# Gating the summed states of a state-space layer on VectorE instead of POOL, for seven of eight sequences

## The chip, the cores and the metric

One core of one Trainium2 chip runs the whole program. The metric is the device time in microseconds of one execution, from the first to the last instruction of the core with what lies around them.

## What is computed

The input holds eight sequences of 256 tokens with 128 features. Each sequence passes four blocks, each one added to its input after a layer norm: a selective state-space layer (Mamba), a mixture of eight experts of which two count for a token, a gated attention, and the same mixture of experts again. The change touches the end of the state-space layer, cut here to its core:

```python
conv = silu(sum(conv_w[k] * xp[:, k:k + T, :] for k in range(4)) + conv_b)
xpj = conv @ xproj_w                       # gives ts, Bm and Cm
delta = softplus(ts @ dt_w + dt_b)
gate_a = silu(gate)                        # gate is the second half of xn @ in_w + in_b
def step(state, inp):                      # one token; 16 states for each of 256 channels
    h_t, d_t, g_t, B_t, C_t = inp
    new = exp(A * d_t) * state + d_t * B_t * h_t
    y = sum over the 16 states of new * C_t, plus D * h_t
    return new, y * g_t
x = x + ssm @ out_w + out_b
```

The product `y * g_t` is what this document calls gating.

## The kernel before, in words

**Tiles.** The channels lie on the 128 partitions in two halves and the 256 tokens along the free axis, so that one tile of a sequence's layer is 128x512 in 32-bit floats. The time recurrence of one state is one scan instruction over such a tile.

**One sequence's states.** For each of the 16 states n of sequence u:

- VectorE (DVE) multiplies delta times h by the broadcast row of B (`dbx`, line 876, written to PSUM) and scans over time (`scan`, line 890, written to the ring `st` of three buffers in SBUF);
- GpSimd (POOL) multiplies the scanned state by the row of C (`mulC`, line 454);
- the product is added up: for sequence 0 on TensorE in PSUM (`NSUM` is 1), for sequences 1 to 7 on POOL in `yacc` in SBUF (`sum_states`, line 467).

`yacc` has two buffers, one for even and one for odd sequences, and is filled first with D times h by ScalarE (`m_y0`).

**After the sixteenth state.** `m_gate` multiplies the sum by `gact`, the silu of the gate half of the projection. For sequence 0 it stands on DVE and reads the sum from PSUM (line 899). For sequences 1 to 7 it stands on POOL (line 474). It counts up the semaphore `m_yg`. TensorE (PE) waits for that in `m_out` (lines 1091 and 1095), the output projection; DVE waits for the projection in `m_res` (line 903), which adds it to `X`. Behind `m_res` stand on DVE the norm of the next block (`n_stats`, line 797, with `n_ve` at line 915; `n_nb`, line 920; `n_lo`, line 927, which writes `xlo`). POOL's `n_pow` (line 413) and ScalarE stand between them. With `xlo` PE can begin the first mixture of experts of the sequence, line 1027. In DVE's queue around this place stand also `combine` (line 991, the weighted sum of experts of an earlier sequence), the first states of the next sequence, and the norm of the sequence after next (`m_stats`, with `m_ve` at line 810, and `m_nb`, line 815), for which POOL takes a power in `m_pow` (line 406).

**The order.** Each engine runs its instructions in order. `build_plan` gives every step of every sequence a planned moment, by tables written out by hand, sorts all steps by it, and each engine emits those steps that it has a function for. The table `M_OUT` plans `m_gate` 2.79, `m_out` 3.4 and `m_res` 5.45 after a common point. The step `m_gate` is in the plan of both DVE and POOL, and a function that returns at once emits nothing.

In the texts below "boundary u" is the place at which sequence u's sum is finished, gated and projected, u from 1 to 7.

Of the kernel before, what the change touches and what calls it, by code (L numbers as in the profile page):

```python
# [5 lines left out]
ALU = mybir.AluOpType  # L6
# [13 lines left out]
NS = 16  # L20
# [14 lines left out]
NSUM = 1  # L35
# [149 lines left out]
def build(nc, x, vecs, in_w, xproj_w, dt_w, out_w, gate_w, up_w, down_w, uv_w, wo_w, row_b, router_w, out):  # L185
    schedule = build_plan()
    norms = norm_order(schedule)
    with ExitStack() as ctx:
        def sb(name, shape, dt=F32):
            return ctx.enter_context(nc.sbuf_tensor(name, shape, dt))  # L190

        def two(bank):
            return bank.rearrange("p (a t) -> p a t", a=2)

        ps = ctx.enter_context(nc.psum_tensor("ps", [P, 8, 512], F32))
        s = {n: ctx.enter_context(nc.semaphore(n)) for n in SEMS}
        bc = nc.dram_tensor("bc", (S, 2 * NS * T), F32).ap()

        rot = [ps[:, k, :] for k in range(NR)]
# [43 lines left out]
        gact = sb("gact", [P, IT, T])  # L243
# [9 lines left out]
        yacc = sb("yacc", [P, 2, IT, T])  # L253
# [45 lines left out]
        def v(col, n=1):  # L299
            return vec[:, col:col + n]  # L300
# [12 lines left out]
        def run_schedule(share):  # L313
            for name, arg in schedule:
                if name in share:
                    share[name](arg)
# [4 lines left out]
        def _(sp):  # L321
            def setup(_):
                def seq(k, n):
                    return x[k * T:(k + n) * T, :].rearrange("(s c p) h -> p (s c) h", c=NC, p=P)

                def tiles(k, n):
                    return X[:, k:k + n].rearrange("p s c h -> p (s c) h")

                sp.dma_start(tiles(0, 1), seq(0, 1)).then_inc(s["d_x0"], 16)
                sp.dma_start(in_raw, in_w).then_inc(s["d_inw"], 16)  # L330
                sp.dma_start(vec[:], vecs).then_inc(s["d_vecs"], 16)
                for sem, dst, src in (("d_xpw", xpw[:], xproj_w), ("d_dtw", dtw[:], dt_w), ("d_outw", outw[:], out_w)):
                    sp.dma_start(dst, src).then_inc(s[sem], 16)
                for k in (0, LOW):
                    sp.dma_start(rowb_raw[k:k + 1, :], row_b).then_inc(s["d_rowb"], 16)
                sp.dma_start(tiles(1, S - 1), seq(1, S - 1)).then_inc(s["d_xs"], 16)
                sp.dma_start(gate_raw, gate_w).then_inc(s["d_gate"], 16)
                sp.dma_start(up_raw, up_w).then_inc(s["d_up"], 16)
                for sem, dst, src in (("d_rw", rw_raw[:], router_w), ("d_uv", uv_raw, uv_w), ("d_wo", wo[:], wo_w)):
                    sp.dma_start(dst, src).then_inc(s[sem], 16)  # L340

            def load_down(_):
                for k in range(NB):
                    rows = min(P, FI - k * P)
                    sp.dma_start(down[0:rows, :, k, :],
                                 down_w[:, k * P:k * P + rows, :].rearrange("e p h -> p e h")).then_inc(s["d_down"], 16)
# [43 lines left out]
        @block.gpsimd  # L390
        def _(pool):
            def setup(_):
                nc.gpsimd.memset(ident[:], 0.0).then_inc(s["w_zero"], 1)
                pool.wait_ge(s["w_zero"], 1)
                nc.gpsimd.affine_select(out=ident[:], in_=ident[:], compare_op=ALU.not_equal, fill=1.0, base=0,
                                        pattern=[[-1, P]], channel_multiplier=1).then_inc(s["w_const"], 1)
                nc.gpsimd.memset(neghalf[:], -0.5).then_inc(s["w_zero"], 1)
                nc.gpsimd.memset(one_at[:], 0.0).then_inc(s["w_zero"], 1)
                nc.gpsimd.iota(iota_i[:], pattern=[[1, NE]], base=0, channel_multiplier=0).then_inc(s["w_iota"], 1)
                pool.wait_ge(s["w_zero"], 3)  # L400
                nc.gpsimd.affine_select(out=one_at[:], in_=one_at[:], compare_op=ALU.not_equal, fill=1.0, base=-RK,
                                        pattern=[[0, 1]], channel_multiplier=1).then_inc(s["w_msk"], 1)

            def m_pow(u):
                pool.wait_ge(s["m_var"], u + 1)
                nc.gpsimd.tensor_tensor(m_r[:], m_ve[:], neghalf[:], ALU.pow).then_inc(s["m_rstd"], 1)

            def n_pow(arg):
                l = norms[arg]
                pool.wait_ge(s["n_var"], l + 1)  # L410
                if l:
                    pool.wait_ge(s["n_xm"], l)
                nc.gpsimd.tensor_tensor(n_r[:], n_ve[:], neghalf[:], ALU.pow).then_inc(s["n_rstd"], 1)  # L413

            def conv_product(k):

                def product(u):
                    if u == 0:
                        return
                    if k == 1:  # L420
                        pool.wait_ge(s["m_pad"], u + 1)
                    if u > 1 or k > 1:
                        pool.wait_ge(s["m_sum"], PAD * (u - 1) + k - 1)
                    w = v(V_CW, IT * KC).rearrange("p (a k) -> p a k", a=IT)[:, :, k:k + 1].broadcast_to([P, IT, T])
                    nc.gpsimd.tensor_tensor(tap[:], xpad[:, :, k:k + T], w, ALU.mult).then_inc(s["m_tap"], 1)  # L425
                return product

            def conv_sum(k):

                def tap_sum(u):  # L430
                    if u == 0:
                        return
                    pool.wait_ge(s["m_tap"], PAD * (u - 1) + k)
                    if k == 1:
                        pool.wait_ge(s["m_tap0"], u + 1)
                    nc.gpsimd.tensor_tensor(conv[:], conv[:], tap[:], ALU.add).then_inc(s["m_sum"], 1)  # L436
                return tap_sum

            def m_delta(u):
                if u == 0:  # L440
                    return
                pool.wait_ge(s["m_pos"], u + 1)
                pool.wait_ge(s["m_ln"], u + 1)
                pool.wait_ge(s["m_dA"], u * NS)
                pool.wait_ge(s["m_dx"], u)
                nc.gpsimd.tensor_tensor(delta[:], sp_e[:], sp_ln[:], ALU.add).then_inc(s["m_delta"], 1)  # L446

            def mulC(arg):

                u, n = arg  # L450
                i = u * NS + n
                pool.wait_ge(s["m_scan"], i + 1)
                row = rowsbc[:, (i // CH) % NCH, n % CH, 1:2, :].broadcast_to([P, IT, T])
                nc.gpsimd.tensor_tensor(st[:, i % NST], st[:, i % NST], row, ALU.mult).then_inc(s["m_p"], 1)  # L454

            def sum_states(arg):

                u, n = arg
                i = u * NS + n
                if u < NSUM:  # L460
                    return
                pool.wait_ge(s["m_p"], i + 1)
                if n == 0:
                    pool.wait_ge(s["m_y0"], u + 1)
                else:
                    pool.wait_ge(s["m_yacc"], i - NS * NSUM)
                nc.gpsimd.tensor_tensor(yacc[:, u % 2], yacc[:, u % 2], st[:, i % NST], ALU.add).then_inc(s["m_yacc"], 1)  # L467

            def m_gate(u):
                if u < NSUM:  # L470
                    return
                pool.wait_ge(s["m_yacc"], (u + 1 - NSUM) * NS)
                pool.wait_ge(s["m_g"], u + 1)
                nc.gpsimd.tensor_tensor(yacc[:, u % 2], yacc[:, u % 2], gact[:], ALU.mult).then_inc(s["m_yg"], 1)  # L474

            run_schedule({"setup": setup, "m_pow": m_pow, "n_pow": n_pow, "m_mul1": conv_product(1), "m_add1": conv_sum(1),
                          "m_mul2": conv_product(2), "m_add2": conv_sum(2), "m_mul3": conv_product(3), "m_add3": conv_sum(3), "m_delta": m_delta, "mulC": mulC,
                          "sum": sum_states, "m_gate": m_gate})

        @block.scalar  # L480
        def _(act):
# [9 lines left out]
            def setup(_):  # L491
                table("exp")
                act.wait_ge(s["d_vecs"], 16)
                nc.scalar.activation(A[:].rearrange("p a n -> p (a n)"), v(V_ALOG, IT * NS), ACT.Exp).then_inc(s["w_A"], 1)
# [241 lines left out]
        def _(dve):  # L736
# [155 lines left out]
                                             op1=ALU.add).then_inc(s["m_scan"], 1)  # L892

            def m_gate(u):
                if u >= NSUM:
                    return
                dve.wait_ge(s["m_ysum"], (u + 1) * NS)
                dve.wait_ge(s["m_g"], u + 1)
                nc.vector.tensor_tensor(yacc[:, u % 2], two(rot[0]), gact[:], ALU.mult).then_inc(s["m_yg"], 1)

            def m_res(u):
                dve.wait_ge(s["m_out"], u + 1)
# [406 lines left out]
```

## Time and profile before

| what | us |
|---|---|
| three timed runs | 674.55, 679.75, 679.70 |
| their median | 679.7 |
| the profiled execution, its own time | 673.82 |
| its span, first to last instruction | 672.2 |
| PE busy | 577.3 |
| DVE busy | 528.1 |
| POOL busy | 399.5 |
| ACT (ScalarE) busy | 383.3 |
| the 112 sums on POOL (line 467) | 143.8 |
| the 128 products with C on POOL (line 454) | 169.0 |

A timeline row has the start and the duration in microseconds, the engine, the line, the operation, what it writes and reads, and in brackets how long the engine sat idle before it and who released it. The chain of waits is followed backward from the last instruction: each piece is what released the next, and "issue" is time that no row explains. The granted clock of TensorE (PEclk) is a share of its full speed: 1.00 is 2.4 GHz, 0.50 is 1.2 GHz, and a value between them is a mean over a stretch that has both.

### The profile page before, as it was taken

What the parts mean: (1) busy time and instruction counts of PE and PEld (TensorE: products, weight loads), DVE (VectorE), ACT (ScalarE), POOL (GpSimd) and SP (SyncE); (2) the same over time, 40 slices, a digit from 0 to 9 for tenths busy, and PEclk for the clock granted to TensorE, in tenths of its full rate; (3) what the DMA queues carried; (4) which work ended last, traced back from release to release, by engine and by line L of the source; (5) the groups of instructions that cost most, each with busy time, mean ns of one, the idle gap of its engine ahead of it and who ended that gap; (6) DMA issues with size and microseconds to landing.
All of it is one profiled execution on the core that took longest, in us unless ns stands there. A gap on an engine that the chain in (4) does not pass through costs nothing.

```text
span 672.2 us, 12730 instructions
## 1 busy us (share of the span) xinstructions
PE 577.3 (86%) x4370; PEld 546.1 (81%) x4370; DVE 528.1 (79%) x1162; ACT 383.3 (57%) x792; POOL 399.5 (59%) x338
## 2 busy tenths in 40 slices
PE   2476792289798999999998999899989999999998
PEld 1222692289798999899898999899988999999998
DVE  6598899667799789988997799978988896545454
ACT  6886565257456675757573765667474641525240
POOL 1296599849667687759674986769775565000000
PEclk9588796569899999989997999999998999999999
DMA  8733033002030303021030303030303000000000
GB/s 294 222 123 125 11 131 119 7 20 120 1 138 9 138 4 137 2 90 59 13 126 14 133 3 138 9 138 3 127 13 121 25 13 1 22 1 13 1 21 9
DMA packets 18163, 45.30 MB, mean 67 GB/s; under 512 B 2800, under 2 KB 13489, under 8 KB 13747
## 3 DMA queue, kind: packets, MB, share of 16 engines
q1 hardware_dynamic: 18098, 44.49, 18.3%
q8 instruction: 35, 0.57, 0.4%
q14 instruction: 30, 0.24, 0.1%
HBM read 40.02 MB, written 1.31 MB: 61 GB/s over the span
## 4 chain that ended last, share of the span: by engine, by line
PE 37%; POOL 35%; issue 15%; DVE 8%; ACT 2%; DMA 1%; SPq 1%; POOLq 0%; DVEq 0%; ACTq 0%
POOL yacc L467 14%; POOL st L454 14%; PE ps L1178 9%; PE ps L1027 7%; PE ps L1028 7%; PE ps L1029 7%; POOL conv L436 2%; POOL tap L425 1%; DVE st L890 1%; DVE X L991 1%; PE ps L1227 1%; DMA inner_ring<-gate_w 1%; POOL delta L446 1%; POOL yacc L474 1%; DVE ps L876 1%
## 5 line engine op out<-in xcount | busy, mean ns | idle before, releaser
L454 POOL TENSOR_TENSOR st<-st,rows_ring 128x512 f32<-128x512 f32 x128 | 169.0, 1321 | 83.3 <-DVE st L890 83.0
L1178 PE MATMUL ps<-down,inner_ring 128*128 128x128 f32 (+1 forms) x1408 | 171.5, 274 | 0.0
L685 ACT ACTIVATE sg<-ps 128x512 f32<-128x512 f32 x176 | 104.6, 596 | 108.4 <-PE ps L1029 102.5
L1178 PEld LDWEIGHTS ps<-down,inner_ring 128*128 128x128 f32 (+1 forms) x1408 | 165.5, 191 | 0.8
L890 DVE TENSOR_TENSOR_SCAN st<-dA,ps 128x512 f32<-128x512 f32 x128 | 155.4, 1214 | 3.4 <-PE ps L1128 0.9
L977 DVE TENSOR_TENSOR inner_ring<-sg,ps 128x512 f32<-128x512 f32 x176 | 118.7, 679 | 49.2 <-ACT sg L685 22.8
L467 POOL TENSOR_TENSOR yacc<-yacc,st 128x512 f32<-128x512 f32 x112 | 143.8, 1284 | 6.4
L1027 PE MATMUL ps<-xhi,gate_hi 128*128 128x256 f32 x352 | 105.1, 299 | 22.2 <-DVE xlo L927 22.2
L640 ACT ACTIVATE dA<-delta,A 128x255 f32<-128x255 f32 x256 | 105.7, 494 | 12.1 <-POOL delta L446 11.9
L1027 PE MATMUL ps<-xhi,up_hi 128*128 128x256 f32 x352 | 105.8, 300 | 0.9 <-DVE inner_ring L977 0.7
L1028 PE MATMUL ps<-xlo,gate_hi 128*128 128x256 f32 x352 | 102.4, 291 | 0.0
L1029 PE MATMUL ps<-xhi,gate_lo 128*128 128x256 f32 x352 | 102.3, 291 | 0.0
L1028 PE MATMUL ps<-xlo,up_hi 128*128 128x256 f32 x352 | 101.8, 289 | 0.0
L1029 PE MATMUL ps<-xhi,up_lo 128*128 128x256 f32 x352 | 101.7, 289 | 0.0
L1027 PEld LDWEIGHTS ps<-xhi,gate_hi 128*128 128x128 f32 x352 | 70.3, 200 | 25.8 <-issue 21.1
L991 DVE SCALAR_TENSOR_TENSOR X<-ps,wts,X 128x128 f32<-128x128 f32 x256 | 75.8, 341 | 19.2 <-PE ps L1178 19.0
L876 DVE TENSOR_TENSOR ps<-ps,rows_ring 128x512 f32<-128x512 f32 x128 | 88.4, 691 | 0.9
L413 POOL TENSOR_TENSOR n_r<-n_ve,neghalf 128x2 f32<-128x2 f32 x24 | 16.6, 693 | 94.0 <-DVE n_ve L915 93.7
L1027 PEld LDWEIGHTS ps<-xhi,up_hi 128*128 128x128 f32 x352 | 69.9, 199 | 2.7 <-DVE inner_ring L977 2.4
L1028 PEld LDWEIGHTS ps<-xlo,gate_hi 128*128 128x128 f32 x352 | 70.5, 200 | 0.1
L1029 PEld LDWEIGHTS ps<-xhi,gate_lo 128*128 128x128 f32 x352 | 70.3, 200 | 0.0
L1028 PEld LDWEIGHTS ps<-xlo,up_hi 128*128 128x128 f32 x352 | 69.9, 199 | 0.1
(145 smaller groups left out, 850.0 us busy)
## 6 DMA issues: line engine op xcount, KB each, us to landing
rows_ring<-bc SPq DMA_DIRECT2D x32, 1024.0 KB, 4.8
moved_rows<-inner_ring SPq DMA_DIRECT2D x96, 32.0 KB, 1.8
inner_ring<-gate_w SPq DMA_DIRECT2D x1, 1408.0 KB, 8.6
inner_ring<-up_w SPq DMA_DIRECT2D x1, 1408.0 KB, 10.9
down<-down_w SPq DMA_DIRECT2D x2, 512.0 KB, 8.9
out<-X SPq DMA_DIRECT2D x8, 128.0 KB, 1.8
X<-x SPq DMA_DIRECT2D x1, 896.0 KB, 5.6
down<-down_w SPq DMA_DIRECT2D x1, 384.0 KB, 8.3
```

The source lines that it names most:

```text
L454: nc.gpsimd.tensor_tensor(st[:, i % NST], st[:, i % NST], row, ALU.mult).then_inc(s["m_p"], 1)
L467: nc.gpsimd.tensor_tensor(yacc[:, u % 2], yacc[:, u % 2], st[:, i % NST], ALU.add).then_inc(s["m_yacc"], 1)
L640: ins = nc.scalar.activation(dA[:, i % NDA, it, 1:], delta[:, it, 1:], ACT.Exp, scale=A[:, it, n:n + 1])
L685: nc.scalar.activation(sg[:, k % 2], two(bank_of(q, 2 * j)), ACT.Silu).then_inc(s["f_sg"], 1)
L876: nc.vector.tensor_tensor(states_in(u, n), dxps, row, ALU.mult).then_inc(s["m_dbx"], 1)
L890: nc.vector.tensor_tensor_scan(out=st[:, i % NST].rearrange(flat), data0=dA[:, i % NDA].rearrange(flat), data1=states_in(u, n).rearrange(f ...
L977: nc.vector.tensor_tensor(inner[:, j], sg[:, k % 2], two(bank_of(q, 2 * j + 1)), ALU.mult).then_inc(s["f_in"], 1)
L991: nc.vector.scalar_tensor_tensor(out=X[:, u, c, :], in0=part, scalar=wts[:, q % 2, c, e:e + 1], in1=X[:, u, c, :], op0=ALU.mult, op1=ALU.a ...
L1027: nc.tensor.matmul(bank, w[0], xv[0], start=start, stop=False)
L1028: nc.tensor.matmul(bank, w[0], xv[1], start=False, stop=False)
L1029: return nc.tensor.matmul(bank, w[1], xv[0], start=False, stop=stop)
L1178: ins = nc.tensor.matmul(bank_of(q, 2 * NP + e)[:, c * H:(c + 1) * H], act_in, down[0:rows, e, n, :], start=n == 0, stop=n == NB - 1)
```

## The change

For sequences 1 to 7 the gating multiplication is taken out of POOL's program and put into DVE's, at the place that the plan gives `m_gate` there. On DVE it waits for all sixteen sums on POOL (`m_yacc`) and for the gate activation (`m_g`), and reads and writes `yacc` in SBUF. Sequence 0 stays as it was.

```diff
--- before
+++ after
@@ POOL
-            def m_gate(u):
-                if u < NSUM:
-                    return
-                pool.wait_ge(s["m_yacc"], (u + 1 - NSUM) * NS)
-                pool.wait_ge(s["m_g"], u + 1)
-                nc.gpsimd.tensor_tensor(yacc[:, u % 2], yacc[:, u % 2], gact[:], ALU.mult).then_inc(s["m_yg"], 1)
-
             run_schedule({"setup": setup, "m_pow": m_pow, "n_pow": n_pow, "m_mul1": conv_product(1), "m_add1": conv_sum(1),
                           "m_mul2": conv_product(2), "m_add2": conv_sum(2), "m_mul3": conv_product(3), "m_add3": conv_sum(3), "m_delta": m_delta, "mulC": mulC,
-                          "sum": sum_states, "m_gate": m_gate})
+                          "sum": sum_states})
@@ DVE
             def m_gate(u):
-                if u >= NSUM:
-                    return
-                dve.wait_ge(s["m_ysum"], (u + 1) * NS)
+                if u < NSUM:
+                    dve.wait_ge(s["m_ysum"], (u + 1) * NS)
+                else:
+                    dve.wait_ge(s["m_yacc"], (u + 1 - NSUM) * NS)
                 dve.wait_ge(s["m_g"], u + 1)
-                nc.vector.tensor_tensor(yacc[:, u % 2], two(rot[0]), gact[:], ALU.mult).then_inc(s["m_yg"], 1)
+                total = two(rot[0]) if u < NSUM else yacc[:, u % 2]
+                nc.vector.tensor_tensor(yacc[:, u % 2], total, gact[:], ALU.mult).then_inc(s["m_yg"], 1)
```

The queues of PE, ScalarE and the DMA issues stay as they are. Lines behind the edit move up by 5 or 7 in the changed kernel.

DVE's queue at boundary 3, before. In it `ps<-delta,h` and `ps<-ps,rows_ring` belong to state 0 of the next sequence, `st<-dA,ps` is the scan, `X<-ps,wts,X` is `combine`, `m_bn`, `m_mv` and `m_ve` are the later norm, and the last row is `m_res`.

```order
L876 TENSOR_TENSOR ps<-ps,rows_ring 128x512 [waits m_scan,d_r1,m_dx]
L991 SCALAR_TENSOR_TENSOR X<-ps,wts,X 128x128 [waits f_x,f_dn]
L991 SCALAR_TENSOR_TENSOR X<-ps,wts,X 128x128 [waits f_x]
L890 SCALAR_TENSOR_TENSOR st<-dA,ps 128x512 [waits m_yacc,m_dbx,m_dA]
L797 BN_STATS m_bn<-X 128x6 x2
L800 BN_AGGR m_mv<-m_bn 128x2 [waits v_chain]
L800 BN_AGGR m_mv<-m_bn 128x2
L810 TENSOR_SCALAR m_ve<-m_mv 128x2 [waits v_chain]
L991 SCALAR_TENSOR_TENSOR X<-ps,wts,X 128x128 [waits f_x,f_dn]
L991 SCALAR_TENSOR_TENSOR X<-ps,wts,X 128x128 [waits f_x]
L903 TENSOR_TENSOR X<-X,ps 128x256 [waits m_out]
```

And the same stretch of DVE's queue in the changed kernel, where `yacc<-yacc,gact` is the gating:

```order
L869 TENSOR_TENSOR ps<-ps,rows_ring 128x512 [waits m_scan,d_r1,m_dx]
L894 TENSOR_TENSOR yacc<-yacc,gact 128x512 [waits m_g,m_yacc]
L986 SCALAR_TENSOR_TENSOR X<-ps,wts,X 128x128 [waits f_x,f_dn]
L986 SCALAR_TENSOR_TENSOR X<-ps,wts,X 128x128 [waits f_x]
L883 SCALAR_TENSOR_TENSOR st<-dA,ps 128x512 [waits m_yacc,m_dbx,m_dA]
L790 BN_STATS m_bn<-X 128x6 x2
L793 BN_AGGR m_mv<-m_bn 128x2 [waits v_chain]
L793 BN_AGGR m_mv<-m_bn 128x2
L803 TENSOR_SCALAR m_ve<-m_mv 128x2 [waits v_chain]
L986 SCALAR_TENSOR_TENSOR X<-ps,wts,X 128x128 [waits f_x,f_dn]
L986 SCALAR_TENSOR_TENSOR X<-ps,wts,X 128x128 [waits f_x]
L898 TENSOR_TENSOR X<-X,ps 128x256 [waits m_out]
```

The gating stands between `dbx` of the next sequence's first state and the next `combine`, with the scan of that state and the later norm behind it. Boundaries 2, 4 and 5 have it between the same two kinds of rows, and boundary 6 too; at boundary 1 it stands between `dbx` and the scan themselves, and at boundary 7 among the rows of `combine` ahead of `m_res`.

POOL's queue at boundary 3, before, where `m_r<-m_ve,neghalf` is `m_pow` and `st<-st,rows_ring` behind it is the product of the next sequence's first state:

```order
L454 TENSOR_TENSOR st<-st,rows_ring 128x512 [waits m_scan]
L467 TENSOR_TENSOR yacc<-yacc,st 128x512 [waits m_yacc,m_p]
L474 TENSOR_TENSOR yacc<-yacc,gact 128x512 [waits m_g,m_yacc]
L406 TENSOR_TENSOR m_r<-m_ve,neghalf 128x2 [waits m_var]
L454 TENSOR_TENSOR st<-st,rows_ring 128x512 [waits m_scan]
L413 TENSOR_TENSOR n_r<-n_ve,neghalf 128x2 [waits n_xm,n_var]
```

And in the changed kernel:

```order
L454 TENSOR_TENSOR st<-st,rows_ring 128x512 [waits m_scan]
L467 TENSOR_TENSOR yacc<-yacc,st 128x512 [waits m_yacc,m_p]
L406 TENSOR_TENSOR m_r<-m_ve,neghalf 128x2 [waits m_var]
L454 TENSOR_TENSOR st<-st,rows_ring 128x512 [waits m_scan]
L413 TENSOR_TENSOR n_r<-n_ve,neghalf 128x2 [waits n_xm,n_var]
```

One row is gone; what follows the last sum is now the power of the later norm.

## Rows read from the trace of the kernel before

**Rows 1.** The page, part 1: busy us (share of the span), instructions.

```profile
PE 577.3 (86%) x4370; PEld 546.1 (81%) x4370; DVE 528.1 (79%) x1162; ACT 383.3 (57%) x792; POOL 399.5 (59%) x338
```

**Rows 2.** The page, part 4: the chain that ended last, by engine.

```profile
PE 37%; POOL 35%; issue 15%; DVE 8%; ACT 2%; DMA 1%; SPq 1%; POOLq 0%; DVEq 0%; ACTq 0%
```

**Rows 3.** The chain around boundary 3: start us, us, what.

```profile
277.52 1.28 POOL yacc L474
...
278.94 0.36 PE ps L1091
...
280.22 0.43 DVE X L903
...
286.73 0.42 DVE xlo L927
...
287.29 0.36 PE ps L1027
```

**Rows 4.** Line 856 alone: duration ns least/median/most, first and last start.

```profile
L856 DVE TENSOR_TENSOR delta<-sp_e,sp_ln x1: 692/692/692, 26.1 to 26.1; 128x512 f32<-128x512 f32 x1
```

**Rows 5.** DVE's timeline at boundary 3.

```profile
275.91 0.68 DVE L876 TENSOR_TENSOR ps<-ps,rows_ring 128x512 f32<-128x512 f32 x1
276.51 0.59 DVE L991 SCALAR_TENSOR_TENSOR X<-ps,wts,X 128x128 f32<-128x128 f32 x2
...
278.93 0.17 DVE L810 TENSOR_SCALAR m_ve<-m_mv 128x2 f32<-128x2 f32 x1
...
280.22 0.42 DVE L903 TENSOR_TENSOR X<-X,ps 128x256 f32<-128x256 f32 x1 [0.61 <-PE ps L1095]
...
281.48 0.17 DVE L915 TENSOR_SCALAR n_ve<-n_mv 128x2 f32<-128x2 f32 x1
```

**Rows 6.** POOL's timeline at boundary 3, behind the gating.

```profile
279.17 0.70 POOL L406 TENSOR_TENSOR m_r<-m_ve,neghalf 128x2 f32<-128x2 f32 x1 [0.38 <-DVE m_ve L810]
279.84 1.27 POOL L454 TENSOR_TENSOR st<-st,rows_ring 128x512 f32<-128x512 f32 x1
```

**Rows 7.** DVE's and POOL's timelines at boundary 2.

```profile
203.21 0.60 DVE L991 SCALAR_TENSOR_TENSOR X<-ps,wts,X 128x128 f32<-128x128 f32 x2
...
207.45 0.42 DVE L903 TENSOR_TENSOR X<-X,ps 128x256 f32<-128x256 f32 x1 [1.13 <-PE ps L1095]
...
204.75 1.27 POOL L474 TENSOR_TENSOR yacc<-yacc,gact 128x512 f32<-128x512 f32 x1
```

**Rows 8.** DVE's and POOL's timelines at boundary 6.

```profile
494.76 0.60 DVE L991 SCALAR_TENSOR_TENSOR X<-ps,wts,X 128x128 f32<-128x128 f32 x2
...
498.46 0.42 DVE L903 TENSOR_TENSOR X<-X,ps 128x256 f32<-128x256 f32 x1 [1.48 <-PE ps L1095]
...
495.77 1.27 POOL L474 TENSOR_TENSOR yacc<-yacc,gact 128x512 f32<-128x512 f32 x1
```

**Rows 9.** The timeline of all engines at boundary 1.

```profile
121.81 1.22 DVE L890 TENSOR_TENSOR_SCAN st<-dA,ps 128x512 f32<-128x512 f32 x1
...
123.40 1.26 POOL L454 TENSOR_TENSOR st<-st,rows_ring 128x512 f32<-128x512 f32 x1
...
123.73 0.96 DVE L810 TENSOR_SCALAR m_ve<-m_mv 128x2 f32<-128x2 f32 x1
...
126.08 1.26 POOL L474 TENSOR_TENSOR yacc<-yacc,gact 128x512 f32<-128x512 f32 x1
...
129.78 0.42 DVE L903 TENSOR_TENSOR X<-X,ps 128x256 f32<-128x256 f32 x1 [5.10 <-PE ps L1095]
```

**Rows 10.** PE's timeline at boundary 7.

```profile
565.72 0.36 PE L1091 MATMUL ps<-rowb,ones_rows 128*128 128x256 f32 x1 [0.19 <-POOL yacc L474]
```

**Rows 11.** Stretches behind xlo: window, us, PE busy, PEclk, DMA share, GB/s.

```profile
287.20:294.20 7.00, 6.91 (x45) 0.76 0.12 30
360.20:367.20 7.00, 6.89 (x33) 0.52 0.09 24
...
572.00:579.00 7.00, 6.78 (x57) 1.00 0.15 41
```

## The prediction

> **What bounds the kernel now.** I read the page first. TensorE (PE) is busy for 86% of the span, DVE for 79%, POOL for 59% [rows 1]. By shares PE should be the bound, but the chain that ended last gives PE 37% and POOL 35% [rows 2]: the end goes back and forth between the two. So the next thing to read is where it changes hands, and one such place is the gating itself. At boundary 3 POOL gates at 277.52, PE begins the projection at 278.94, DVE adds it to X at 280.22, DVE has xlo at 286.73, and PE begins the next mixture of experts at 287.29 [rows 3]. From 280.22 to 286.73 the pieces of the chain are DVE's, nearly without a gap. The same happens at boundaries 1 to 6, so what moves `m_res` (line 903) on DVE moves the next stretch of PE, and with that everything behind it. The question is therefore not whether POOL or DVE is busier, but when `m_res` starts.
>
> **What is removed.** Seven multiplications of POOL, 1.28 us each [rows 3], 9.0 us of its busy time. Not much of that was in POOL's own way. What POOL does next is the power `m_pow` and the product of the next sequence's first state; at 279.17 it had sat idle 0.38 us for `m_ve` of DVE [rows 6]. Seven times 1.28 is no gain by itself.
>
> **What is added.** Seven multiplications on DVE. The nearest row is the one 128x512 tensor_tensor from SBUF and SBUF to SBUF that DVE runs, 0.692 us [rows 4]. The following instruction starts about 0.60 us after such a one, as 276.51 after 275.91 shows [rows 5]. By itself that is 4.2 us of DVE, and it ends 0.6 us sooner than POOL's 1.28: PE could project 0.6 us earlier at each boundary.
>
> **What is added as a wait.** The gating can't start before POOL has landed the sixteenth sum, and this moment is the one at which POOL's own gating started: 277.52. DVE comes to its place before that. Queued behind it on DVE are a `combine`, the scan of the next sequence's state 0, the later norm up to `m_ve`, another `combine`, and then `m_res`. All of them are delayed, whether they need the sum or not, and POOL's `m_pow` and first product wait for them.
>
> The sum for boundary 3: the `combine` that started at 276.51 [rows 5] now starts at 277.52 + 0.60 = 278.12, 1.61 us later (1.01 of waiting, 0.60 of work). Ahead of `m_res` DVE had been idle 0.61 us [rows 5], waiting for the projection. The projection now comes 0.6 us earlier and is no longer the last to arrive; DVE itself is. So `m_res` moves by 1.61 - 0.61 = **+1.00 us**. The other boundaries by the same working:
>
> - Boundary 2: 204.75 + 0.60 - 203.21 = 2.14, less the idle 1.13 [rows 7]: +1.0.
> - Boundaries 4 and 5 have the pattern of boundary 3 (1.60 less 0.60, 1.61 less 0.61): +1.0 each.
> - Boundary 6: 495.77 + 0.60 - 494.76 = 1.61, less 1.48 [rows 8]: +0.1.
> - Boundary 1: the scan of 121.81 waits until 126.08 + 0.60, 4.87 later, less the idle 5.10 [rows 9]: -0.2. It can't gain over 0.6, which is what the projection gains.
> - Boundary 7: the idle time on DVE is long and nothing of a next sequence is queued; PE had waited only 0.19 for the gating [rows 10], so the faster gating gives -0.2.
>
> Together: 1.0 x 4 + 0.1 - 0.2 - 0.2 = **+3.7 us**.
>
> **A second price, on POOL and DVE together.** With `m_ve` 1.6 us later, POOL's first product runs from about 281.4 to 282.7 instead of from 279.84 [rows 6], and `n_ve`, 1.0 later than 281.48 [rows 5], falls at 282.5, inside it. At boundary 1 such a small DVE instruction took 0.96 us instead of 0.17, and it ran until POOL's product of 123.40 had ended [rows 9, 5]. So `n_ve` may be held until POOL is through: 0.2 us at boundary 3 and about as much at 4 and 5; at 2 and 6 the product ends before. I take 3 x 0.2 = +0.6. The bounds are 0 and seven times the 0.79 of boundary 1, 5.5 us; I stay near the first, because the held time is only what is left of one POOL instruction at a moment that I can work out.
>
> The Trainium skill has a rule for this ("GPSIMD Engine Reference", section Specifications): POOL's SBUF interfaces are shared with VectorE, with contention when VectorE's instruction is in a two-port mode or has two SBUF inputs. The gating on DVE has two SBUF inputs, so the rule speaks against the change: by it each gating could be held by a POOL instruction, at most 1.28 us x 7 = 9.0 us more, and the sum would be +13.3. The 0.96 us of boundary 1 agrees with the rule. But here the two instructions next in POOL's queue wait for `m_ve` and for the scan, both behind the gating on DVE, so POOL stands still while DVE gates; by rule and row together the gating costs 0.69.
>
> **The sum:** +3.7 + 0.6 = +4.3 us. On the profiled execution: 673.82 + 4.3 = 678.1 us. The timed runs have a median of 679.7, 5.9 above that execution, with one run near it (674.55) and two at the median; a kernel with the same habit would show 679.7 + 4.3 = **684.0 us**, which I forecast. It is +0.6%, less than the 1% that a measurement of this kernel can tell from no change.
>
> **Rival A, the clock (slower).** PE's clock falls to 1.2 GHz behind these boundaries. In 7 us behind xlo the mean granted clock is 0.76 at boundary 3, 0.52 at boundary 4 and 1.00 at boundary 7 [rows 11]. A stretch that falls from 0.76 to 0.52 loses 7 x 0.24 = 1.7 us on PE, which is the chain there. The change makes PE idle longer at boundaries 2 to 5 (1 us more each, part of it before the gate half of the projection, which needs `m_res`). If three of the four stretches of the 0.76 kind become 0.52, that is +5.0 on top of +4.3: +9.3, 689.0 us. For it: boundary 4 had the longest wait for xlo and the longest slow stretch, boundary 7 the shortest and none. Against: boundaries 2, 5 and 6 wait for xlo by different lengths and have nearly the same mean clock as boundary 3, so a little more idle time need not tip one.
>
> **Rival B, the shorter gating decides (faster).** If DVE's delayed work has slack that I don't see, so that `m_res` follows the projection as before, each boundary gains what the gating is shorter by: 1.28 - 0.69 = 0.59, at boundary 7 only 0.19. That is 6 x 0.59 + 0.19 = -3.7, 676.0 us. For it: PE waits for the gating at every boundary, and DVE had idle time ahead of `m_res` at each. Against: it decides only where that idle time is over 1.6 us or so, and at boundaries 2 to 6 it is 0.61 to 1.48 [rows 5, 7, 8]. It holds in full at boundaries 1 and 7 alone.
>
> **Rival C, the delay is absorbed (no change).** The delayed start of PE's stretch finds slack later: for instance, POOL's conv and sums of the next sequence would have been waiting anyway for something that doesn't move. Then only a part arrives at the end: about +0.5, 680.2 us. For it: the chain passes between engines and a near second chain is not shown. Against: PE's stretch, DVE's scans and POOL's products of the next sequence are all delayed by the same microsecond, so there is no engine on which the next boundary would be early.
>
> **How the numbers follow.** Forecast +4.3: 0.55. Its own range is 676.5 to 687, from the lower group of timed runs plus 2 to the upper plus 7. Rival A 0.2, rival B 0.07, rival C 0.18. The range for the 8 in 10 is 677 to 689: the low end is the lowest timed run with rival C or with half of the forecast, the high end is rival A. Slower by over 1% is above 686.5: most of rival A, and the tail of the forecast if the second price is nearer its upper bound, 0.22. Faster by over 1%, below 672.9, would need more than rival B gives, 0.03. The rest is 0.75.
>
> **What would show it right or wrong.** In the profile after, DVE should have seven rows of the gating of 0.69 us with an idle of about 1.0 us before them at boundaries 3 to 6, 1.5 at boundary 2 and 4.3 at boundary 1, released by POOL's sum. The wait of `m_res` for the projection should be gone at boundaries 2 to 5. PE's wait for the gating should shrink by 0.6 us, and a new wait for `m_res` of about 1 us should stand ahead of the gate half of the projection. The distance from POOL's last sum to the start of the experts (line 1027) should grow by 1.0 at boundaries 2 to 5. `n_ve` should last longer at boundaries 3 to 5. I am wrong if that distance doesn't grow, if it grows and the period of a sequence doesn't, or if the granted clock behind xlo changes more than the distance does.

## The result, and the profile after

The changed kernel has a median of 683.15 us (679.4 to 688.9, 20 runs), the kernel before 677.19 us (674.0 to 680.4, 20 runs). The ratio is 1.0099, with a 95% interval from 1.0073 to 1.0126: it is slower by 0.99%, about 6.7 us (6.0 by the medians). The profiled execution has a span of 679.6 us, 7.4 more than before.

The page of the changed kernel, busy times and the chain that ended last, for [rows 1, 2]:

```profile
PE 583.2 (86%) x4370; PEld 549.4 (81%) x4370; DVE 531.7 (78%) x1169; ACT 385.0 (57%) x792; POOL 390.9 (58%) x331
...
PE 47%; POOL 24%; DVE 11%; issue 9%; ACT 2%; DVEq 0%; POOLq 0%; ACTq 0%
```

POOL lost 8.6 us of busy time and DVE gained 3.6. Neither number is the change of the span, and PE, on which nothing was edited, is busy for 5.9 us more with the same 4370 matmuls. That is the first sign that more than one thing happened.

DVE's timeline at boundary 3 in the changed kernel, for [rows 5]:

```profile
279.48 0.68 DVE L869 TENSOR_TENSOR ps<-ps,rows_ring 128x512 f32<-128x512 f32 x1
281.04 0.69 DVE L894 TENSOR_TENSOR yacc<-yacc,gact 128x512 f32<-128x512 f32 x1 [0.88 <-POOL yacc L467]
281.65 0.60 DVE L986 SCALAR_TENSOR_TENSOR X<-ps,wts,X 128x128 f32<-128x128 f32 x2
...
284.07 0.17 DVE L803 TENSOR_SCALAR m_ve<-m_mv 128x2 f32<-128x2 f32 x1
284.15 0.61 DVE L986 SCALAR_TENSOR_TENSOR X<-ps,wts,X 128x128 f32<-128x128 f32 x2
284.68 0.41 DVE L898 TENSOR_TENSOR X<-X,ps 128x256 f32<-128x256 f32 x1
...
285.93 0.36 DVE L910 TENSOR_SCALAR n_ve<-n_mv 128x2 f32<-128x2 f32 x1
```

The gating is there with 0.69 us, behind 0.88 us in which DVE waits for POOL's last sum. `m_res` (line 898 now) has no bracket any more: it waits for nothing, DVE itself is late. `n_ve` takes 0.36 instead of 0.17 us. POOL in the same stretch, for [rows 6], stands still until DVE has `m_ve`:

```profile
279.74 1.27 POOL L467 TENSOR_TENSOR yacc<-yacc,st 128x512 f32<-128x512 f32 x1
284.32 0.70 POOL L406 TENSOR_TENSOR m_r<-m_ve,neghalf 128x2 f32<-128x2 f32 x1 [3.31 <-DVE m_ve L803]
```

The chain of waits there, for [rows 3]: POOL's sum, then only DVE, then PE.

```profile
279.74 1.28 POOL yacc L467
...
284.76 0.34 DVE X L898
...
291.37 0.42 DVE xlo L922
...
291.93 0.36 PE ps L1022
```

**The distance.** For each boundary I take the time from the end of POOL's last sum to the start of PE's first matmul of the experts behind xlo. At boundary 3 that is 291.93 - 281.01 = 10.92 us; before it was 9.85, with the sum's end at 277.44. All seven, from the same rows at each boundary:

| boundary | 1 | 2 | 3 | 4 | 5 | 6 | 7 | sum |
|---|---|---|---|---|---|---|---|---|
| before | 10.92 | 10.60 | 9.85 | 10.73 | 9.83 | 9.85 | 7.99 | 69.8 |
| after | 10.79 | 11.47 | 10.92 | 11.92 | 11.05 | 9.85 | 7.59 | 73.6 |
| predicted change | -0.2 | +1.0 | +1.2 | +1.2 | +1.2 | +0.1 | -0.2 | +4.3 |
| measured change | -0.1 | +0.9 | +1.1 | +1.2 | +1.2 | 0.0 | -0.4 | +3.8 |

So the distances give +3.8 us. They have two parts. The start of `m_res`, counted from the end of the sum, moves by -0.6 us at boundary 1, by +0.88 or +0.89 at boundaries 2 to 5, by 0.0 at 6 and by -0.4 at 7. From `m_res` to the experts it takes 0.2, 0.3 and 0.3 us longer at boundaries 3 to 5, where `n_ve` is held, and 0.5 us longer at boundary 1. There the instruction that is held is another, `m_b` of the later norm, which now begins inside POOL's first product and ends with it. First DVE before, then POOL and DVE after:

```profile
130.72 0.15 DVE L815 SCALAR_TENSOR_TENSOR m_b<-m_mv,m_r 128x2 f32<-128x2 f32 x1
```

```profile
130.58 1.28 POOL L454 TENSOR_TENSOR st<-st,rows_ring 128x512 f32<-128x512 f32 x1
...
131.23 0.64 DVE L808 SCALAR_TENSOR_TENSOR m_b<-m_mv,m_r 128x2 f32<-128x2 f32 x1
```

So the small change at boundary 1 is a gain of 0.6 and a loss of 0.5.

From the end of the first boundary's sum to the end of the span the kernel before needs 546.2 us and the changed one 552.5: +6.3. (The other 1.1 us of the 7.4 come ahead of that sum, where no instruction was moved.) 2.5 us are open.

**The clock.** The granted clock in the ten microseconds from the start of the experts at boundaries 2 to 7, first the kernel before, then the changed one. Columns: window, its length, PE busy, PEclk, DMA share, GB/s.

```profile
215.30:225.30 10.00, 9.92 (x69) 0.83 0.09 25
287.30:297.30 10.00, 10.00 (x71) 0.83 0.12 32
360.30:370.30 10.00, 9.99 (x60) 0.67 0.08 21
433.80:443.80 10.00, 9.96 (x71) 0.83 0.11 31
505.50:515.50 10.00, 9.87 (x68) 0.83 0.11 28
572.20:582.20 10.00, 9.89 (x81) 1.00 0.13 35
```

```profile
217.30:227.30 10.00, 9.91 (x57) 0.66 0.08 21
291.90:301.90 10.00, 9.97 (x71) 0.83 0.12 31
366.10:376.10 10.00, 9.97 (x64) 0.73 0.09 25
440.40:450.40 10.00, 10.00 (x61) 0.69 0.10 27
513.40:523.40 10.00, 9.90 (x69) 0.83 0.11 28
579.60:589.60 10.00, 9.91 (x81) 1.00 0.14 35
```

PE is busy all the time in these stretches and is the chain. The clock that is missing, (1 - PEclk) x 10 us added over the six, is 10.1 us before and 12.6 us after: +2.5. At boundary 2 in the changed kernel 57 matmuls fall into the ten microseconds where 69 did before. The open 2.5 us stand just there: from the start of the experts to the end of the next boundary's sum the changed kernel takes 1.55 us more behind boundary 2, 0.5 less behind boundary 4 and 1.3 more behind boundary 5, and behind the others at most 0.15 more. That is +2.5, and with the distances' 3.8 it makes the 6.3. One profile can't say how much of this the change brings on every time. At boundary 6, whose distance is 9.85 to 9.89 us in all profiles without spare matmuls, the missing clock is 1.7 us before, 3.4 in e3_work_two_sbuf and e4_gate_behind_scan and 0 in e5_dve_2to5.

PE's waits from 205 to 572 us, first the one for the gating in the kernel before, then the changed kernel. Columns: who waited for whom, us in total, times, longest.

```profile
PE ps L1091 <- POOL yacc L474: 5.3, 6, 1.1
```

```profile
PE ps L1022 <- DVE xlo L922: 16.1, 10, 2.6
PE ps L1022 <- DVE X L898: 2.7, 4, 0.7
PE ps L1017 <- ACT n_xn L644: 2.5, 4, 0.9
PE ps L1086 <- DVE yacc L894: 2.0, 5, 0.5
```

The wait for the gating is down from 1.1 to 0.5 us at most, as foretold. Two waits are new in this stretch: for `m_res` ahead of the gate half of the projection (four times, 0.7 at most), and for the norm ahead of its transposes (four times). PE's idle time is broken up otherwise and is about 2 us longer, 24.3 instead of 22.4.

### The profile page after: what moved, and what is told of

Its sections match the earlier page's. It is cut to its first block, busy times and chain, and to the rows that moved or that the text cites. A ratio compares the mean times of both kernels' runs of the same rounds, so it can differ in the third digit from the quotient of the medians.

```text
span 679.6 us, 12730 instructions
## 1 busy us (share of the span) xinstructions
PE 583.2 (86%) x4370; PEld 549.4 (81%) x4370; DVE 531.7 (78%) x1169; ACT 385.0 (57%) x792; POOL 390.9 (58%) x331
## 4 chain that ended last, share of the span: by engine, by line
PE 47%; POOL 24%; DVE 11%; issue 9%; ACT 2%; DVEq 0%; POOLq 0%; ACTq 0%
PE ps L1173 12%; PE ps L1022 10%; POOL yacc L467 10%; POOL st L454 10%; PE ps L1023 9%; PE ps L1024 9%; DVE st L883 2%; DVE X L986 2%; POOL conv L436 2%; PE ps L1222 2%; POOL delta L446 1%; DVE ps L869 1%; DVE n_b L915 1%; POOL tap L425 1%; DVE n_bn L790 1%
## 5 line engine op out<-in xcount | busy, mean ns | idle before, releaser
L1024 PEld LDWEIGHTS ps<-xhi,up_lo 128*128 128x128 f32 x352 | 70.1, 199 | 0.0
## 6 DMA issues: line engine op xcount, KB each, us to landing
inner_ring<-up_w SPq DMA_DIRECT2D x1, 1408.0 KB, 11.6
```

What stands on the lines that cost most here:

```text
L1024: return nc.tensor.matmul(bank, w[1], xv[0], start=False, stop=stop)
```

## The experiments

Three theories were put against each other. **The wait:** DVE is held until POOL's last sum, and what is queued behind comes later. **The work:** every added DVE instruction costs. **The collision:** a DVE instruction with two SBUF inputs and a POOL instruction hold each other up. The clock was then tested by itself. In the table, "distances" is the sum of the seven changes as above, "clock" the missing clock of the six stretches of ten microseconds (10.1 before), and "from the first sum" the time from the end of boundary 1's sum to the end of the span, against 546.2 before; these three are of one profiled execution each. Each ratio is to the kernel before as it was timed in the same series; e1 to e4, e5 to e8 and e9 to e12 are three series on three chips. The same kernel came out at 0.9920 in one of them (e7) and at 0.9867 in another (e10), so that a difference of 0.3% between two series proves nothing.

| run | timed ratio (95%) | distances | clock | from the first sum |
|---|---|---|---|---|
| changed kernel | 1.0099 (1.0073 to 1.0126) | +3.8 | 12.6 | +6.3 |
| e1_wait_only | 1.0074 (1.0043 to 1.0104) | +1.9 | 11.9 | +3.7 |
| e2_work_only | 1.0038 (1.0014 to 1.0062) | +0.9 | 11.9 | +2.5 |
| e3_work_two_sbuf | 1.0026 (1.0002 to 1.0051) | +0.1 | 10.2 | +1.8 |
| e4_gate_behind_scan | 0.9967 (0.9942 to 0.9993) | -1.0 | 11.8 | +0.4 |
| e5_dve_2to5 | 1.0110 (1.0081 to 1.0139) | +4.4 | 13.6 | +8.5 |
| e6_dve_167 | 1.0036 (1.0015 to 1.0056) | +0.6 | 11.9 | +2.4 |
| e7_fill_before | 0.9920 (0.9890 to 0.9950) | -0.4 | 0.0 | -6.6 |
| e8_fill_after | 0.9931 (0.9899 to 0.9962) | +3.4 | 0.0 | -4.1 |
| e10_fill_before_again | 0.9867 (0.9837 to 0.9898) | -0.4 | 0.0 | -6.6 |
| e11_fill_after_again | 0.9899 (0.9867 to 0.9931) | +3.3 | 0.0 | -4.0 |
| e9_behind_scan_fill | 0.9926 (0.9900 to 0.9952) | -1.4 | 1.7 | -5.8 |
| e12_fill_boundary_1 | 0.9843 (0.9808 to 0.9878) | -1.1 | 0.0 | -10.2 |

### e1_wait_only: the wait without the work

```diff
             def m_gate(u):
                 if u >= NSUM:
+                    dve.wait_ge(s["m_yacc"], (u + 1 - NSUM) * NS)
                     return
```

> POOL gates as before; DVE only waits, at the place of the changed kernel's gating, for POOL's last sum, and does no multiplication. Theory (the wait holds back what is queued behind it on DVE): at boundary 3 DVE is held 1.0 us, less the 0.61 it had idle ahead of m_res, so m_res and the start of the experts come 0.4 us later; the same at 2, 4 and 5, up to 0.2 more where n_ve is held by POOL's product; nothing at 1, 6, 7. Sum +1.6 to +2.4 us, with a lengthened slow clock stretch up to +4. Rival (it is the added DVE work that costs): 0. Rival (two SBUF inputs collide with POOL): 0.

DVE's timeline at boundary 3 of e1_wait_only:

```profile
278.81 0.69 DVE L876 TENSOR_TENSOR ps<-ps,rows_ring 128x512 f32<-128x512 f32 x1
280.37 0.61 DVE L992 SCALAR_TENSOR_TENSOR X<-ps,wts,X 128x128 f32<-128x128 f32 x2 [0.88 <-POOL yacc L467]
```

DVE is held 0.88 us with nothing to do at the end of it. The distances grow by 0.3, 0.5, 0.6 and 0.6 us at boundaries 2 to 5 and by nothing at 1, 6 and 7: +1.9, in the foretold range, where both rivals said 0. The timed loss of 0.74% is 5.0 us, more than the +4 that I had allowed; its interval, 2.9 to 7.0, has the 3.7 of the profile in it. A wait alone costs half of the change's distances. At boundary 3 `m_res` comes 0.29 us later, which is the wait of 0.88 less the 0.61 that DVE had idle ahead of `m_res`.

### e2_work_only and e3_work_two_sbuf: the work without the wait

```diff
                 row = rowsbc[:, g % NCH, n % CH, 0:1, :].broadcast_to([P, IT, T])
+                if n == 0 and u > 1:
+                    mark(nc.vector.tensor_tensor(dbxps, dxps, two(gate_hi[:, 0:2 * T].bitcast(F32)), ALU.mult))
+                    link()
```

e3_work_two_sbuf has `two(gate_lo[:, 0:2 * T].bitcast(F32))` in the place of `dxps`.

> POOL gates as before; DVE runs, ahead of the first state's product of sequences 2 to 7 (boundaries 1 to 6), one more 128x512 multiplication with one PSUM and one SBUF input, whose result is overwritten: work without the wait, about 0.75 us with its own ordering. Theory: it is covered by DVE's idle time ahead of m_res (0.61 to 5.1 us), so at most +0.15 at boundaries 3 to 5, sum about +0.5 us. Rival (added DVE work costs): 6 x 0.75 = +4.5 us.

> As e2_work_only, but the added multiplication has two SBUF inputs, and it falls while POOL is computing its last product and sum. If two SBUF inputs collide with POOL: its row is longer than 0.69 us (up to 0.69 + 1.3), or a POOL row beside it is 1.7 instead of 1.28; POOL's last sum comes up to 0.7 us later at each of six boundaries: +1 to +5 us. Without a collision: as e2_work_only, +0.5 us.

In e2_work_only the distances grow by 0.2, 0.35 and 0.4 at boundaries 3 to 5 and not at all at 1, 2, 6 and 7, where DVE had over 1 us of idle time: +0.9. That is twice the foretold 0.5, and nearly all of it is `n_ve`, 0.36 us at boundary 3 here too and 0.50 at 4 and 5, because the delayed `m_ve` puts POOL's product on top of it. `m_res` itself comes at most 0.04 us later. The work theory said +4.5 and falls. The timed +0.38% (2.6 us) is again more than the distances; in the profile the rest is one longer slow stretch of the clock, behind boundary 3.

The two experiments together give the change. At boundary 3 the wait of 0.88 and the work of 0.60 stand against 0.61 us of idle time: alone each is covered wholly or for the most part (0.29 and 0.03 us are left), together they move `m_res` by 0.89.

In e3_work_two_sbuf the collision is seen. Line 877 alone is the added multiplication (duration in ns, least, median, most):

```profile
L877 DVE TENSOR_TENSOR ps<-gate_lo,gate_hi x6: 691/740/1632, 122.8 to 496.2; 128x512 f32<-128x512 f32 x6
```

POOL's timeline of e3_work_two_sbuf has the last sum of boundary 3:

```profile
276.91 1.60 POOL L467 TENSOR_TENSOR yacc<-yacc,st 128x512 f32<-128x512 f32 x1
```

The multiplication takes up to 1.63 us where that of e2_work_only, with one of its inputs in PSUM, took 0.68 to 0.70 in all six, and POOL's last sum takes 1.60 to 1.62 instead of 1.27 to 1.28 at boundaries 2 to 6. So two SBUF inputs and POOL do hold each other up. The distances don't show what that costs, because they begin at the end of the sum. Five times 0.33 us is 1.65, and this with the +0.1 of the distances is the +1.8 from the first sum. It lies in the range of +1 to +5 that stood for a collision, and the timed +0.26% is 1.8 us too. That e2_work_only is not faster in spite of it comes of its own +0.9 of distances and its longer slow stretch. In the changed kernel itself all seven gatings took the undisturbed time, as line 894 alone shows:

```profile
L894 DVE TENSOR_TENSOR yacc<-yacc,gact x7: 692/693/693, 127.2 to 572.1; 128x512 f32<-128x512 f32 x7
```

The collision is no part of the gating's own cost, because POOL has nothing it could run at that moment. It does cost at the small instructions behind it, `n_ve` at boundaries 3 to 5 and `m_b` at boundary 1.

### e4_gate_behind_scan: the same work one place further back

```diff
+                if late:
+                    m_gate(late[0])
+                    late.clear()
+
+            late = []
 
             def m_gate(u):
+                if 1 <= u <= 6 and not late:
+                    late.append(u)
+                    return
                 if u < NSUM:
                     dve.wait_ge(s["m_ysum"], (u + 1) * NS)
```

The first piece stands at the end of `scan`.

> The changed kernel with the gating on DVE moved one place back at boundaries 1 to 6: behind the scan of the next sequence's first state, which DVE does while POOL finishes the last sum. Theory (the wait is what costs): no wait at boundaries 3 to 6, m_res where it was before the change (0.0), at boundaries 1 and 2 up to 0.6 earlier, at 7 0.4 earlier: about -1.5 us against the kernel before. Rival (added DVE work costs): still +4 us. Rival (two SBUF inputs against POOL): here POOL has its first product ready while DVE gates, so the row of the gating is longer than 0.69 or POOL's product is held.

DVE's timeline at boundary 3 of e4_gate_behind_scan:

```profile
279.41 1.20 DVE L883 TENSOR_TENSOR_SCAN st<-dA,ps 128x512 f32<-128x512 f32 x1
280.53 0.66 DVE L902 TENSOR_TENSOR yacc<-yacc,gact 128x512 f32<-128x512 f32 x1
281.12 0.47 DVE L790 BATCH_NORM_STATS2 m_bn<-X 128x6 f32<-128x128 f32 x2
```

The gating has no wait ahead of it. The distances are 10.3, 10.1, 9.9, 10.9, 10.1, 9.9 and 7.6, together 1.0 less than before, and the timed ratio is 0.9967: the same seven multiplications on the same engine (the one of boundary 7 at its old place), and the loss is gone. The gain of 1.5 us that I expected is met by the distances' 1.0 and the timed 2.2 (0.5 to 3.9) only roughly. From the first sum the profile is even 0.4 us longer, with a longer slow stretch behind boundary 6. This is the strongest point against the work theory, and it says what was wrong with the change: not the engine, but the place in DVE's queue, one scan too early. Without the wait the work of 0.60 is covered by the idle time of 0.61.

### e5_dve_2to5 and e6_dve_167: the change in two halves

The condition in both `m_gate` functions was cut to `2 <= u <= 5` in the one and `u in (1, 6, 7)` in the other, for example:

```diff
@@ DVE
-                if u >= NSUM:
+                if u >= NSUM and not (2 <= u <= 5):
                     return
```

> Gating on DVE for sequences 2 to 5, on POOL for 1, 6 and 7. Theory (the cost lies where DVE had less idle time ahead of m_res than it is now held): all of the loss, distances from last sum to the experts +0.9, +1.1, +1.2, +1.2 = +4.4 us, in the timed runs up to +7 with longer slow clock stretches. Rival (each of seven added multiplications costs the same): 4/7 of the loss, about +3.5.

> The complement: gating on DVE for sequences 1, 6 and 7 only. Theory: distances -0.1, 0.0, -0.4, so -0.5 us or no change. Rival (each multiplication costs the same): 3/7 of the loss, about +2.7.

e5_dve_2to5 has the whole loss, 1.0110, with distances of +0.9, +1.1, +1.2 and +1.2, as foretold. Its +8.5 from the first sum is more than that of the changed kernel, because 13.6 us of clock are missing behind these four boundaries instead of 10.9. e6_dve_167 did not come out: I expected no loss, and it is slower by 0.36%, nearly the 0.4% of the rival. Its profile has two reasons at a boundary where nothing was moved. Boundaries 1, 6 and 7 have -0.1, 0.0 and -0.4, at boundary 1 with the 0.5 us of the held `m_b` in it. But boundary 3, where POOL gates as before, has +1.1. The timeline of all engines there, in e6_dve_167:

```profile
283.38 1.27 POOL L467 TENSOR_TENSOR yacc<-yacc,st 128x512 f32<-128x512 f32 x1
...
283.55 1.12 DVE L815 SCALAR_TENSOR_TENSOR m_b<-m_mv,m_r 128x2 f32<-128x2 f32 x1
```

The instruction ahead of `m_b`, the `dbx` of line 876, started 0.30 us late, and I found no wait that explains it. With that, `m_b`, a 128x2 instruction with two SBUF inputs, fell into POOL's sum and lasted until its end. In all the other runs it takes 0.14 or 0.15 us there. The second reason is a longer slow stretch of the clock behind it. Whether most of the timed executions of e6_dve_167 have this, one profile can't tell; it stays open.

### e7 to e11: the clock

```diff
                 if j == 0:
+                    if QUEUE[q][1] == 1 and 2 <= QUEUE[q][0] <= 6:
+                        for _ in range(12):
+                            nc.tensor.matmul(two(bank_of(q, 0))[:, 0], gate_hi[:, 0:P], gate_hi[:, 0:T], start=True, stop=True)
                     pe.wait_ge(s["n_lo"], norms["q", q] + 1)
```

> The kernel before, with twelve spare 128x256 matmuls on TensorE (1.3 us at full clock) in the wait for xlo at boundaries 2 to 6, into the bank that the next real matmul starts anew. If TensorE's idle time there is what lets its clock fall, the slow stretches behind xlo (20.5 us at half clock in the profile before) go or shrink, up to -10 us. If not, no change, or up to +0.5 us where the spare matmuls overrun the wait.

> The same spare matmuls in the changed kernel. If the part of the loss beyond the distances (about 2 to 3 us of 6) is the clock, and the spare matmuls hold the clock up, then this kernel is slower than e7_fill_before by the distances alone, +3.8 to +4.3 us. If they don't hold it up, by the full +6 us.

PE's timeline at boundary 3 of e7_fill_before; line 1150 are the spare matmuls:

```profile
288.26 1.68 PE L1150 MATMUL ps<-gate_hi 128*128 128x256 f32 x12
290.36 0.39 PE L1027 MATMUL ps<-xhi,gate_hi 128*128 128x256 f32 x1 [0.42 <-DVE xlo L927]
```

PE waits 0.42 us there instead of 1.94 in the profile before. The granted clock of the ten microseconds behind it, boundaries 2 to 4 of e7_fill_before:

```profile
218.60:228.60 10.00, 9.91 (x83) 1.00 0.12 32
290.40:300.40 10.00, 10.00 (x81) 1.00 0.12 31
362.10:372.10 10.00, 9.97 (x84) 1.00 0.12 33
```

It is 1.00 in these and the other three. The clock that was missing there was 10.1 us, and from the first sum the profile is 6.6 us shorter; the timed runs gain 0.8%. So it is PE's idle time just ahead of xlo that lets the clock fall, and it can be bought off with matmuls that compute nothing. (At boundary 4 1.1 us of idle time are left, and the clock holds.)

The Trainium skill ("TensorE: Matmul & The Clock Gate", section "HAM oscillation — how this bites in real kernels") tells this for waits on DMA: the engine idles and comes back at the lower clock, and the work should be arranged so that it doesn't wait in between. The trace agrees, with a wait on VectorE in place of the DMA, and a granted clock of 1.00 instead of 0.83 at boundary 3 where the wait of 1.94 us is filled.

With the clock held in both kernels, the changed one (e8_fill_after, median 672.54) is 0.9 us slower than e7_fill_before (671.63). That is far less than 6 and also less than the +3.8 to +4.3 that I had expected. Both were run again:

> e7_fill_before again, beside e8's kernel in the same series, because six and eight runs left the difference of the two open between 0 and 4 us. Expected 0.992 to the kernel before.

> e8_fill_after again. If the distances alone are left of the loss (+2.5 to +3.8 us by the profiles of e7 and e8): slower than e10_fill_before_again by 2.5 to 3.8 us, ratio 0.996 to the kernel before. If the loss is all clock: no difference to e10.

Medians of 669.00 and 670.26 us, +1.3, where I had said +2.5 to +3.8; in the profiles, from the first sum, +2.5 and +2.6. Both kernels came out lower than expected, 0.9867 and 0.9899 instead of 0.992 and 0.996. The means of the two pairs differ by 1.5 and 2.1 us, with six to eight runs of each kernel that spread over 3 to 6 us, so the timed runs don't tell 1 from 2.6. In the timed runs, then, the larger part of the 6.7 us goes with the clock. In the profiles it is the smaller part, 2.5 of 6.3, and the distances still differ by 3.8 with the clock held. How the timed loss divides stays open. Why the profiles' +2.6 is below the distances' 3.8 can be seen: both profiles of the kernel with the spare matmuls but without the change have one slow stretch of clock in the middle of sequence 3's states, which neither profile with the change has. There, between the experts of boundary 2 and the sum of boundary 3, the kernel with the change is 1.3 us faster. e7_fill_before first, then e8_fill_after:

```profile
255.00:265.00 10.00, 8.83 (x62) 0.83 0.06 16
```

```profile
255.00:265.00 10.00, 8.72 (x75) 1.00 0.03 9
```

### Two versions that beat both kernels

> The gating on DVE behind the scan (e4_gate_behind_scan) together with the spare matmuls of e7_fill_before. If the two effects are separate, the gains add: -2 us of the first and -5 us of the second, a ratio near 0.989 to the kernel before. If the spare matmuls gain only by hiding what the place of the gating does, no better than e7_fill_before, 0.992.

0.9926 (0.9900 to 0.9952), median 672.07: no better than e7_fill_before, and 3 us slower than the same kernel in its own series (e10, 669.00). The 2 us of e4_gate_behind_scan did not add to the spare matmuls. Its distances are 1.0 shorter than those of e10, but one stretch at boundary 4 fell to a clock of 0.83. I can't settle from one profile whether that is chance.

The last version adds spare matmuls at boundary 1: the 66 shown here, and the twelve ahead of xlo, for which the condition above becomes `1 <= QUEUE[q][0] <= 6`. The rest is as in e9_behind_scan_fill.

```diff
                 free("mamba")
+                if u == 1:
+                    pe.wait_ge(s["m_yacc"], 12)
+                    for _ in range(66):
+                        nc.tensor.matmul(mambaps[:, 0:T], gate_hi[:, 0:P], gate_hi[:, 0:T], start=True, stop=True)
                 pe.wait_ge(s["m_yg"], u + 1)
```

> e9_behind_scan_fill with spare matmuls at boundary 1 too: 66 of them behind the twelfth sum of sequence 1 while TensorE waits for the gating, and twelve in the wait for xlo. The profile before has the clock at half from about 10 us ahead of the gating to 144 us, with TensorE busy at half clock for some 7 us behind xlo. If it holds the clock up there, 3 to 8 us less than e9_behind_scan_fill; if TensorE's gaps between 127 and 137 us let it fall again, no change.

0.9843 (0.9808 to 0.9878), median 666.72: the fastest of all, 11.6 us below the median of the kernel before in the same series (678.31) and 5.4 below e9, in the foretold 3 to 8. (In the profile before the clock is at half from 107.5 us, 18.6 us ahead of the gating and not some 10.) Three stretches around boundary 1, first e9_behind_scan_fill, then e12_fill_boundary_1:

```profile
112.00:127.00 15.00, 0.00 (x0) 0.50 0.19 70
127.00:140.00 13.00, 8.34 (x33) 0.50 0.01 1
140.00:155.00 15.00, 15.00 (x106) 0.82 0.34 121
```

```profile
112.00:127.00 15.00, 8.99 (x54) 0.61 0.20 71
127.00:140.00 13.00, 8.23 (x49) 0.76 0.00 0
140.00:155.00 15.00, 15.00 (x122) 0.98 0.41 150
```

PE had idled ahead of that boundary for 22 us, and paid for it in the next 20. Now 122 matmuls fall into the third stretch instead of 106.

## Why the prediction was right, and where it was not

- **What bounds:** right. `m_res` on DVE sets the next stretch of PE. In all runs the distance follows what DVE does between POOL's sum and xlo: up to `m_res` first, and behind it where a small instruction is held.
- **The added wait, +3.7 without `n_ve`:** right in kind and nearly in size. `m_res` was foretold 1.00 us later at boundaries 2 to 5 and came 0.88 or 0.89 later; DVE waited 0.88 us there instead of 1.01. The seven distances were foretold within 0.2 us each (+4.3 with `n_ve`, measured +3.8). At boundary 1 that is luck: -0.2 was foretold and -0.1 measured, but `m_res` came 0.6 us earlier, and the held `m_b`, for which the sum had nothing, took 0.5 of it back. e1_wait_only and e4_gate_behind_scan show that it is the wait and the place, and e5_dve_2to5 that it sits at boundaries 2 to 5.
- **The removed POOL time is no gain:** right. POOL stood still 3.31 us behind its last sum instead of gating.
- **The second price, `n_ve` held by POOL's product:** right. 0.36 us instead of 0.17 at boundary 3 and 0.50 at boundaries 4 and 5, together +0.8 against the foretold +0.6. e3_work_two_sbuf and e6_dve_167 show the collision at up to 1.63 and 1.12 us, and it was right to leave it out of the gating's own price, 0.69 in all seven. The rule of the Trainium skill on the interfaces that POOL and VectorE share ("GPSIMD Engine Reference", section Specifications) agrees with the rows of e3_work_two_sbuf and with `m_b`, which have two SBUF inputs. `n_ve`, and `m_ve` with its 0.96 us in the prediction, have one; whether they fall under the rule's other case, the two-port mode, no row shows.
- **The sum of +4.3 us:** too small; the ratio's interval is +4.9 to +8.5 us. The step that failed is the treatment of the clock as a separate rival with all or nothing, so that the sum had it at 0. It was one more term: 2.5 of the 6.3 us in the profile, and 1.8 and 1.6 us in the profiles of e1_wait_only and e2_work_only. Rival A named the mechanism and the place. It said three stretches would get longer; two did (boundaries 2 and 5) and one got shorter (boundary 4).
- **The absolute time:** 684.0 foretold and 683.15 measured, but partly by luck. I built on a median of three runs, 679.7, while that of twenty is 677.19. The first group of timed runs was high by 2.5 us, and my sum was low by 1.7 (6.0 by the medians, 4.3 foretold).
- **Rivals B and C:** both fall. The shorter gating decides only at boundaries 1 and 7, where `m_res` comes 0.6 and 0.4 us earlier, and nothing absorbed the delay: no stretch between the experts and the next sum got shorter but the one behind boundary 4, where less clock was missing.

## What to carry to other kernels

In an in-order queue everything behind a moved instruction is delayed by the wait it brings and by its own work, less the idle time that stood there anyway (0.88 + 0.60 - 0.61 us at boundary 3): read that idle time at the next instruction that waits for the same chain, and put the moved one as far back as its result allows. The same seven multiplications cost 6.7 us at one place and nothing with six of them one scan later. Look also at what small instructions the delay pushes into a long one of POOL: two such cases, `n_ve` and `m_b`, cost 1.3 us here. And where TensorE is the chain behind a wait, a microsecond more of idling may cost as much again in its clock (1.55 us behind boundary 2, where the distance had grown by 0.9), though not each time; a few spare matmuls in the wait are a cheap test of it.

## What the runs showed of the hardware

- The first boundary's sum ended at 126.0 us in the profile before and between 126.6 and 131.1 in the others, though almost nothing had been edited ahead of it. It goes with the clock of that part: PEclk from 60 to 126 us was 0.73 to 0.76 in the four profiles with the latest sum (e2, e4, e7 and e8, 129.4 to 131.1) and 0.78 to 0.82 in the others. The timed runs of the kernel before range over 6.4 us, so that a difference of 2 us needs the start taken out of the profiles, or many timed runs.
- A DVE instruction of two columns with two inputs in SBUF took 1.12 us when it began 0.17 us into a 128x512 sum on POOL (`m_b`, boundary 3 of e6_dve_167), and 0.64 us when it began in the middle of a product (boundary 1 of the changed kernel). At boundary 3 of all other profiles it began before POOL's sum, in the second half of a 128x2 power, and took 0.14 or 0.15.
- The other way round, a 128x512 sum on POOL took 1.60 to 1.62 us instead of 1.27 beside a 128x512 multiplication on DVE with two SBUF inputs, and 1.27 to 1.28 beside one with an input in PSUM (e3_work_two_sbuf, e2_work_only).
- Twelve spare matmuls per boundary, 60 in all, took 0.8 to 1.3% off a kernel that was computing the same.
